# Fused gated cross-attention stack on one core: VectorE's transposes behind the next scores' minima, and strips copied for each pair of score tiles

## The reference

```python
def _L3_xattn_ref(x, latents, mask, g1, b1, g2, b2, Wq, Wkv, Wout):
    heads, dim_head = (16, 64)
    xn = layer_norm(x, g1, b1)            # the context, 512 tokens
    ln_lat = layer_norm(latents, g2, b2)  # the stream, 512 tokens
    q = ln_lat @ Wq
    kv = jnp.concatenate([xn, ln_lat], axis=1) @ Wkv    # 1024 keys
    k, v = jnp.split(kv, 2, axis=-1)
    ...
    weight = jnp.einsum('bhld,bhnd->bhln', q * scale, k * scale)
    weight = jnp.where(full_mask[:, None, None, :], weight, neg)
    weight = jax.nn.softmax(weight.astype(jnp.float32), axis=-1).astype(q.dtype)
    out = jnp.einsum('bhln,bhnd->bhld', weight, v)
    out = out.transpose(0, 2, 1, 3).reshape(b, l, heads * dim_head)
    return out @ Wout
...
x = x + jnp.tanh(g_xattn[3]) * _L3_xattn_ref(ctx_1024, _layernorm(x, axis=-1), mask_BxS2_bk0, ...)
```

## Time and profile before

| | |
|---|---|
| median of three runs | 3193.31 us (3190.65 to 3195.45) |
| the profiled execution | 3195.45 us, span 3193.7 us, mean granted PE clock 0.888 |
| PE matmul busy | 2507.8 us, 79% of the span |
| VectorE / ScalarE / GpSimd busy | 1884.2 us (59%) / 1120.5 us (35%) / 787.8 us (25%) |
| the four stages of the changed function, with their last values | 293, 295, 294 and 285 us |
| copies of `move` | 768 by SP, 256 by ScalarE, 128 KB each |

### The profile page before, as it was taken

One profiled execution on the slowest core, in us unless ns is written; L12 is line 12 of the kernel. 1 busy time (PEld: TensorE's weight loads), 2 busy tenths in 40 slices (PEclk: granted clock), 3 DMA queues, 4 the chain that ended last, 5 costly groups with the idle time before them and its releaser, 6 DMA issues. The chain is left out here.

```text
span 3193.7 us, 34077 instructions
## 1 busy us (share of the span) xinstructions
PE 2507.8 (79%) x11904; PEld 1301.9 (41%) x11904; DVE 1884.2 (59%) x4079; ACT 1120.5 (35%) x2015; POOL 787.8 (25%) x494
## 2 busy tenths in 40 slices
PE   6899943847877898777899778789867878987885
PEld 2334321314444445333544434344533444453343
DVE  5677741147866662577584367768247667635664
ACT  1434411212332341444352244435134434414442
POOL 1003354410000230233241033324013323202331
PEclk8999966875979799999999889999989999999998
DMA  7411055752101102355400255530125551013553
GB/s 227 113 28 29 14 147 161 265 209 89 60 7 52 48 1 80 79 132 126 138 1 7 81 117 121 132 106 8 43 78 125 126 126 60 7 67 83 129 132 86
DMA packets 113976, 290.52 MB, mean 91 GB/s; under 512 B 37222, under 2 KB 57318, under 8 KB 107786
## 3 DMA queue, kind: packets, MB, share of 16 engines
q1 hardware_dynamic: 93210, 243.85, 26.9%
q10 hardware_dynamic: 13424, 35.94, 4.5%
q0 software_dynamic: 7168, 8.50, 0.9%
HBM read 119.81 MB, written 29.74 MB: 47 GB/s over the span
## 5 line engine op out<-in xcount | busy, mean ns | idle before, releaser
L820 POOL TENSOR_SCALAR pbuf<-pbuf,recip 128x1024 f32<-128x1024 f32 x128 | 364.5, 2847 | 1168.0 <-DVE recip L738 1168.0
L679 PE MATMUL ps<-kH,qT 64*128 64x512 f32 x1024 | 317.0, 747 | 205.6 <-ACT pbuf L780 202.9
L780 ACT ACTIVATE pbuf<-ps,least 128x1024 f32<-128x1024 f32 x256 | 285.3, 1115 | 500.6 <-DVE least L731 500.6
L744 DVE STREAM_TRANSPOSE pbuf<-pbuf 128x2048 f32<-128x2048 f32 x128 | 295.8, 2311 | 242.6 <-POOL pbuf L820 147.1
L731 DVE CUSTOM_DVE_ANT_0 ps<-ps,mask 128x1024 f32<-128x1024 f32 x256 | 304.3, 1230 | 39.0 <-PE ps L679 38.9
L587 POOL TENSOR_SCALAR pbuf<-pbuf,recip 128x512 f32<-128x512 f32 x128 | 200.2, 1576 | 452.2 <-DVE recip L508 452.2
L679 PEld LDWEIGHTS ps<-kH,qT 64*128 64x128 f32 x1024 | 103.3, 217 | 336.4 <-ACT pbuf L780 248.2
L693 PE MATMUL ps<-work,vh 128*64 128x256 f32 x2048 | 236.8, 384 | 2.3 <-ACT wide L792 2.3
L558 ACT ACTIVATE pbuf<-ps,least 128x512 f32<-128x512 f32 x256 | 172.7, 686 | 159.4 <-DVE least L498 159.1
L1465 ACT ACTIVATE early<-ps 128x1536 f32<-128x1536 f32 x86 | 124.0, 1441 | 199.8 <-PE ps L1298 199.8
L1538 DVE TENSOR_REDUCE mh<-ps 128x3 f32<-128x1536 f32 x86 | 150.0, 1744 | 68.0 <-PE ps L1287 67.3
(11 more groups left out here) (343 smaller groups left out, 3906.8 us busy)
## 6 DMA issues: line engine op xcount, KB each, us to landing
work<-pbuf SPq DMA_DIRECT2D x768, 128.0 KB, 2.5
work<-pbuf ACTq DMA_DIRECT2D x256, 128.0 KB, 4.0
early<-in_L_wgu SPq DMA_DIRECT2D x24, 768.0 KB, 6.4
expert_rows<-zero_rows SPq DMA_DIRECT2D x16, 1024.0 KB, 11.5
yg<-expert_rows SPq DMA_DIRECT2D x16, 1024.0 KB, 6.3
early<-in_L_wd SPq DMA_DIRECT2D x24, 384.0 KB, 7.7
arena<-in_L_wo SPq DMA_DIRECT2D x8, 1024.0 KB, 10.2
arena<-in_L_wff SPq DMA_DIRECT2D x4, 2048.0 KB, 9.4
```

What stands on the lines that cost most here:

```text
L679: last = nc.tensor.matmul(scores(n)[:, kb * BANK:(kb + 1) * BANK], q_of(g, s, qt), k_of(g, s, kb), start=True, stop=True)
L744: nc.vector.transpose(x, x).then_inc(turned, 1)
L780: nc.scalar.activation(unit(n), scores(n).rearrange("p (j r) -> p j r", j=strips), ACT.Exp, bias=least[:, n % 8:n % 8 + 1], scale=-1.0, ac ...
L820: nc.gpsimd.tensor_scalar(unit(n), unit(n), recip[:, n % 8:n % 8 + 1], None, mult).then_inc(pool_divided, 1)
```

## The change

VectorE does turn(p) after find(2p+2), find(2p+3) and invert(2p+2) instead of before them, and keeps both units' jobs after invert(2p+3). The copies are made for each pair: 16 for a pair, each 2 KB from each of 32 partitions, with 4 slots of one pair in `probs`, in `pts` and in `moved`. PE does `values` ahead of both units' jobs. The jobs' slots become (2, 3, 4, 5, 6).

```diff
-    moved = [sem(name + f"_moved_{i}") for i in range(2)]
+    moved = [sem(name + f"_moved_{i}") for i in range(4)]
...
     def unit(n):
-        return probs[n // 4 % 2][:, :, n // 2 % 2, n % 2, :]
+        return probs[n // 2 % 4][:, :, n % 2, :]
...
         def values(h):
             g, half = divmod(h, 2)
-            pe.wait_ge(moved[h % 2], arrivals * (h // 2 + 1))
+            for p in (2 * h, 2 * h + 1):
+                pe.wait_ge(moved[p % 4], arrivals * (p // 4 + 1))
...
-                                            pts[half][:, :, :, s, c, :].rearrange("p a t q -> p t a q"),
+                                            pts[:, 2 * half:2 * half + 2, :, s, c, :].rearrange("p t a q -> p (t a) q"),
...
             if p + 1 < N:
                 score(p + 1)
-            for job in before[2 * p]:
-                project(job)
             if p >= 4 and p % 2 == 0:
                 values(p // 2 - 2)
-            for job in before[2 * p + 1]:
-                project(job)
+            for n in (2 * p, 2 * p + 1):
+                for job in before[n]:
+                    project(job)
...
         for p in range(N):
-            turn(p)
             if p + 1 < N:
                 find(2 * p + 2)
                 find(2 * p + 3)
                 invert(2 * p + 2)
-            keep_jobs(2 * p)
+            turn(p)
             if p + 1 < N:
                 invert(2 * p + 3)
+            keep_jobs(2 * p)
             keep_jobs(2 * p + 1)
 
-    def move(eng, h, diagonal):
-        eng.wait_ge(turned, 2 * h + 2)
-        if h >= 2:
-            eng.wait_ge(av_ready, h - 1)
+    def move(eng, p, diagonal):
+        eng.wait_ge(turned, p + 1)
+        if p >= 4:
+            eng.wait_ge(av_ready, p // 2 - 1)
...
-            if p >= 4 and n % 4 == 0:
-                act.wait_ge(moved[p // 2 % 2], arrivals * (p // 4))
+            if p >= 4 and n % 2 == 0:
+                act.wait_ge(moved[p % 4], arrivals * (p // 4))
...
-            if p % 2:
-                move(act, p // 2, True)
+            move(act, p, True)
...
     def mover(sp):
-        for h in range(N // 2):
-            move(sp, h, False)
+        for p in range(N):
+            move(sp, p, False)
...
-                         sums, recip, least, wide, jobs3, (0, 2, 4, 5, 6), 3)
+                         sums, recip, least, wide, jobs3, (2, 3, 4, 5, 6), 3)
```

More of the change, by code:

```diff
@@ L742, in turn @@
             v.wait_ge(act_divided, p + 1)
-            x = probs[p // 2 % 2][:, :, p % 2, :, :].rearrange("p j s r -> p j (s r)")
+            x = probs[p % 4].rearrange("p j s r -> p (j s r)")
             nc.vector.transpose(x, x).then_inc(turned, 1)
@@ L767, in move @@
                 if (a == j) == diagonal:
-                    eng.dma_start(pts[h % 2][32 * j:32 * (j + 1), a, :, :, :, :].rearrange("p t s c q -> p (t s c q)"),
-                                  probs[h % 2][32 * a:32 * (a + 1), j, :, :, :].rearrange("p t s r -> p (t s r)"))                        .then_inc(moved[h % 2], 16)
+                    eng.dma_start(pts[32 * j:32 * (j + 1), p % NT, a, :, :, :].rearrange("p s c q -> p (s c q)"),
+                                  probs[p % 4][32 * a:32 * (a + 1), j, :, :].rearrange("p s r -> p (s r)"))\
+                        .then_inc(moved[p % 4], 16)
     def scalar(act, background={}):
@@ L2858, in layers2to3 @@
                          lambda g, s, c: vh[g % 2][:, c, s * DH2:(s + 1) * DH2], mask3[:, :],
-                         [pbuf[:, 4 * i:4 * i + 4, :].rearrange("p j (t s r) -> p j t s r", t=2, s=2) for i in range(2)],
-                         [work[:, i * 4096:(i + 1) * 4096].rearrange("p (x c q) -> p x c q", c=8, q=32)
-                          .rearrange("p (a t s) c q -> p a t s c q", a=4, t=2) for i in range(2)],
-                         sums, recip, least, wide, jobs3, (0, 2, 4, 5, 6), 3)
+                         [pbuf[:, 2 * i:2 * i + 2, :].rearrange("p i (x r) -> p (i x) r", r=256)
+                          .rearrange("p (j s) r -> p j s r", s=2) for i in range(4)],
+                         work[:, :].rearrange("p (t x) -> p t x", t=NT).rearrange("p t (a x) -> p t a x", a=4)
+                         .rearrange("p t a (s c q) -> p t a s c q", s=2, c=8),
+                         sums, recip, least, wide, jobs3, (2, 3, 4, 5, 6), 3)
         def l3_tensor(pe, background={}):
```

## The result

The changed kernel takes 3246.93 us at the median of four runs (3243.56 to 3257.95), the kernel before 3194.38 beside it (3190.65 to 3196.73): ratio 1.0172, 95% interval 1.0144 to 1.0200, slower by 52.6 us. The forecast, 3217, has the sign, and its range of 3166 to 3252 holds the time, but it gave 24 us where 52.6 were measured.

What follows compares the result with a forecast made beforehand. No engine was full, so order and waits set the length. Steps gave -32 us and PE's clock +56: +24 on the profiled 3195.45, 3219, or 3217 us at the median; range 3166 to 3252.

Steps and rivals of the forecast that it cites:

- A: Loop step of pair p mod 4 = 0, score start to next score start: 7.9 us before, forecast 6.3 through ScalarE's issues.
- B: Step of p mod 4 = 1, with q and keys 0 in one pair: 7.9 us before, forecast 11.2 at full clock.
- D: Step of p mod 4 = 3, bare chain of score, find and exponential: 6.6 us before, forecast 4.75.
- C: Step of p mod 4 = 2, PE's scores, values, keys 1, its copy, vals 0: 10.9 us before, forecast 10.2.
- clock's price: PE's slow products after its idle in B: 2.0 us per group taken, bounds 0 and 3.0, 28 x 2.0 = +56.
- Rival 1: Faster, as the slow clock costs B only 0.6 us per group: 3178, down to 3154 us; chance 0.29.
- Rival 2: No change, with the clock's price near 1.1 us per group: 3193 us; chance 0.13.
- Rival 3: SP's copy queue becomes the bound at 9.0 us a pair, 36.0 a group, +67: 3258 us; chance 0.08.
- Rival 4: Transposes slowed beside GpSimd's division, 3.05 instead of 2.31 us, +41: 3258 us; chance 0.05.
- 24 groups: Middle six groups of four pairs in each stage: 32.5 us against 33.6 each, -26 in all before the clock's price.
- first four pairs: Start of each stage: 30.5 us against 31.2, four stages -3 before the clock's price; vals 0 taken as 2.0.
- last pairs and end: Last pairs of a stage: -3 us kept in stage four, 0 in the other three, their two jobs as in B.

Runs made afterwards that it cites:

- e2: Changed kernel with five throwaway PE products put in the pause behind q: ratio 1.0077 to the kernel before, four stages 1193.8 us.
- e4: Changed kernel with VectorE's copy of unit 2p's job (q in B) moved ahead of the transpose: ratio 0.9870 to the kernel before, four stages 1114.2 us.
- e1: Changed kernel with the old slots (0, 2, 4, 5, 6): ratio 0.9780 to the kernel before, four stages 1102.4 us.
- e11: Changed kernel with old slots, early copy of q and ScalarE's copy issues later: ratio 0.9778 to the kernel before, four stages 1094.4 us.
- e8: Changed kernel with background norm jobs moved so that two of three lie in B: ratio 1.0123 to the kernel before, four stages 1219.5 us.
- e7: Kernel before with only the new slots (2, 3, 4, 5, 6): ratio 1.0201 to the kernel before, four stages 1245.5 us.
- e0: Changed kernel run again, unedited, as reference: 3323.74 us against 3266.72 for the kernel before, ratio 1.0177, four stages 1222.1 us.
- e6: Changed kernel with VectorE's old order and the old slots, leaving copies by pair and values first: ratio 1.0096 to the kernel before, stages 1199.4 us.
- e5: Kernel before with only VectorE's new order, transpose behind finds and first reciprocal: ratio 0.9922 to the kernel before, four stages 1142.6 us.
- e9: Changed kernel with the old slots and q's copy ahead of the transpose: ratio 0.9773 to the kernel before, four stages 1109.6 us.

## Why the prediction was right or wrong

**Right, step by step.** The 2.87 us of the division left the loop. (Of the kernel before, A and B took 8.7 and 7.1 to 7.3 at the mean; the 7.9 and 7.9 of the prediction are one group's, with the same sum.) D came out at 4.6 to 4.8 (4.75 forecast), A at 6.48 in stage four (6.3), where ScalarE's issues hold the exponential; B at 13.1 (11.2 + 2.0). C at 10.56 (10.2) holds part of the clock's price, that of its own score block, which I had booked in B. A whole group of stage four took 34.74 where I had 34.5, as B and D came out a little under the forecast and A and C over it. The clock's price was 3.66 - 1.98 + 2.44 - 1.99 = 2.1 us per group, against 2.0 taken. e2 shows that filling the pause takes back more than half of it, e4 that a shorter pause does, and e1 that without the pair of slots the rest gains 64.

**The rivals.** Rival 1, no price for the clock: 27 of the 28 keys blocks took over 3 us. Rival 2, no change: out of the interval. Rival 3, SP's queue: SP waited for a transpose in 62 of its 128 turns, 227.0 us in all, so it wasn't full in this kernel (in e11 it is). By its own terms, 28 x 2.4 on 3193, it would have given 3260, not 3258. Rival 4, the port: transposes took 2300 to 2312 ns throughout. The instruction that it was priced from, 0.90 us for 0.16, had met a division begun 0.22 us before; the same one took 0.16 in the midst of a division (1385.80, where the division runs from 1384.43 to 1387.27). The Trainium skill (SBUF — State Buffer, "Who interferes with whom") has a VectorE instruction with one SBUF input outside the 2-port modes not contend with GpSimd, and that agrees: 2.31 us at 2985.51, beside a division that runs from 2985.68 to 2988.52.

**Where it failed.** The mechanism was right; three terms of the sum that I had set by the plain case were mis-sized, which makes 34 of the 43 us by which the profiled executions miss the forecast:

| term | forecast | measured |
|---|---|---|
| 24 groups | -26 + 24 x 2.0 = +22 | 6 x (1.57 + 1.54 + 2.17 + 1.43) = +40.3 |
| first four pairs, four stages | -3 + 4 x 2.0 = +5 | 139.1 - 126.5 = +12.6 |
| last pairs and end | -3 | +5.1 |
| outside the stages | 0 | +8.8 |
| sum, profiled executions | +24 | +66.9 |

- *Groups, 18 us short.* In stage four a group is 0.24 over the forecast, which makes 24 x 0.24 = 5.8 if all stages share it. The other 13 or so is "I take the two middle stages as the first", or rather that I worked out new steps from a stage without background and used them for all; two thirds of it lie in A (6.8, 6.9 and 7.2 in stages one to three, 6.5 in stage four). Before, VectorE's small background jobs ran in its wait for GpSimd; that wait was their cover. With it gone, they stand in front of `find` (2.17 us at 1377.22; A 7.1 instead of 6.5 at two places of each of these stages). But e8 shows that this isn't all: with the jobs elsewhere those two places take 6.5, but the groups stay at 35.2, and long issues of ScalarE sit in A (four in 4.26 us and an A of 8.1, in place of 2.6 and 6.5). In the changed kernel four issues take over 2.9 us at 3, 5 and 4 places of stages one to three and at 1 of stage four, and 1, 2, 2 and 0 of these hold an A of the middle groups, the longest 4.49 us with an A of 8.4; why they come stays open.
- *First four pairs, 8 us short.* "vals 0 2.0": without values in step C of the first group, PE has a second pause, 3.76 us before vals 0, which then takes 3.6 to 3.7. I charged the clock once for each group and not at that place: the step takes 11.8 to 12.1 where I had 9.8, and the others of the four are as forecast in three of the stages.
- *Last pairs, 8 us short.* "both behind the transpose, as in B: 0". The likeness to B was right and the price not: if they are as in B, they cost as B does. Three stages gave +2.1, +2.7 and +2.1, stage four -1.8; e4, which takes their copies ahead of the transpose, has the three pairs at 22.2 to 22.8 us instead of 26.8 in those stages.
- *Outside the stages*, 8.8 us in the profiled run are in code that wasn't touched. The difference of the medians, 52.6, is smaller than that of the stages, and the profiled executions of one set of experiments differ by 9 to 24 us outside the stages, so I count them as scatter between executions; their cause isn't shown.

**Of the edits.** The slots are what makes the change lose: +79 alone (e7), +120 on the rest (e0 against e1). Copies by pair with the values ahead lose 33 under the old order (e6) and gain 40 under the new one; VectorE's order alone gains 24 (e5). I had put B at 11.2 + 2.0 and D, A and C together 4 to 5 us below before, so the forecast held this trade; what I didn't do is to price the parts apart, which might have shown a version 2% faster than before, one edit away from the changed kernel (e1).

## What to carry to other kernels

When a wait goes away, list what ran inside it: small jobs on the same engine, DMA issues, another engine's slack. Each needs its price in the stage where it occurs, not in the cleanest one. Where two products share one PSUM bank, the copy between them is on TensorE's path, so put that copy ahead of any long instruction of its engine: here one moved line was worth 110 us. And a slower TensorE clock is to be charged at every place that gets a long pause, the first and the last turns of a loop too, for a filled pause there is often filled by work that these turns lack.

## What the runs showed of the hardware

- Slow products came after quite short pauses: 3.13 us before a 3.78 us keys block (e7) and 3.11 before a 3.79 us score block (e9), while one of 2.66 had left a block at 1.99. But the length of the pause doesn't decide it. In e7 the pause before keys 0 was 3.12 to 3.13 us at 17 places, and the block took 3.78 at 11 of them and 1.98 at 6; in e4 it was 3.21 to 3.44 at 17 places, with 1.98 or 1.99 at 6 and 2.7 to 3.8 at the others. A fast block of each (e7 in stage one, e4 in stage four):

```profile
1411.80 1.98 PE L2811 MATMUL ps<-arena 128*128 128x512 f32 x4 [3.13 <-DVE qT L2614]
...
3069.69 1.98 PE L2811 MATMUL ps<-arena 128*128 128x512 f32 x4 [3.22 <-DVE qT L2614]
```

- With products of 64 rows in the pause and 1.5 to 1.7 us idle left (e2), the next block came out at 1.98 at one place and at 3.59 at another.
- An issue by ScalarE holds its next exponential: four of 64 KB take 2.5 us of its time, 4.49 at the slowest place, and four of 128 KB beside SP's take 3.66 (e5). SP's issues cost 591 ns at the median for 64 KB and 592 for 128 KB (0.61 and 0.68 us at the mean), so half the size costs nearly twice as much per byte. From issue to landing took 2.0 us at the median for SP's smaller and 2.5 for its larger ones, 2.1 and 4.0 for ScalarE's.
- A 32 x 32 transpose of 128 x 2048 takes 2.31 us beside a GpSimd division, the same as without it.
